# Four-layer graph network: one layer's count tables kept in DRAM for another layer, and a difference of two weights

## The reference

```
# L0, relation: 64 edge types
msg = (x[src] + rel_emb[type64]) @ W_msg.T + b_msg
agg = segment_sum(msg, dst) / max(deg, 1)
# L1, weighted attention, 4 heads: sums over edges grouped by src, weight edge_weight
# L2, typed: 2 edge types, 0 = data, 1 = control
m_data = Xs @ W_data.T + b_data           # Xs = X[src]
m_ctrl = Xs @ W_control.T + b_control
msg = where(type2 == 0, m_data, m_ctrl)
out = relu(segment_sum(msg, dst) + X @ W_self.T + b_self)
# L3, plain: h = x @ W.T + b, sums of norm * h[col] over edges and self loops
```

## Time and profile before

| what | us |
|---|---|
| median of three runs | 6132.15 (6131.38 to 6135.97) |
| the profiled execution | 6133.85 |
| its span in the profile | 6132.1 |
| sorting the edges, constants, L0's own projections (start to about 2256) | 2256 |
| L0: own stage | 2311 to 3084 |
| L1: own stage | 3173 to 4318 |
| L2: own stage, with its tail to 5524 | 4404 to 5501 |
| L3: own stage | 5568 to 6120 |

### The profile page before, as it was taken

How to read it: one execution, slowest core, us unless ns; L and a number is a source line. 1 busy time by engine, 2 the same in 40 slices (tenths; PEclk the granted TensorE clock), 3 DMA queues, 4 the chain that set the end, 5 groups by cost and what they waited for, 6 DMA issues and landing times. The chain is left out here.

```text
span 6132.1 us, 121790 instructions
## 1 busy us (share of the span) xinstructions
PE 5401.7 (88%) x44062; PEld 4317.7 (70%) x44063; DVE 4755.8 (78%) x12715; ACT 2193.0 (36%) x3365; POOL 1557.8 (25%) x1592
## 2 busy tenths in 40 slices
PE   4888888888888859999959999999699999997998
PEld 3666666666666646767659999999577777765666
DVE  7777777777777777788879999999555555557888
ACT  0111111111111114445423333333366666655665
POOL 0577777777777740000000000000000000000000
PEclk9999999999999989999979999999799999998999
DMA  2100000000000010000000000000000000000000
GB/s 79 24 2 2 2 2 2 2 2 2 2 2 2 2 35 4 2 1 2 1 3 1 1 1 1 1 1 1 2 1 1 1 1 1 1 1 2 7 8 10
DMA packets 60237, 33.64 MB, mean 5 GB/s; under 512 B 51583, under 2 KB 54097, under 8 KB 59598
## 3 DMA queue, kind: packets, MB, share of 16 engines
q1 hardware_dynamic: 8622, 22.14, 1.2%
q0 software_dynamic: 50176, 3.31, 0.9%
q10 hardware_dynamic: 1056, 2.86, 0.2%
HBM read 13.67 MB, written 14.54 MB: 5 GB/s over the span
## 5 line engine op out<-in xcount | busy, mean ns | idle before, releaser
L1391 ACT ACTIVATE gC<-qC 128x768 bf16<-128x768 f32 (+3 forms) x1960 | 1614.3, 824 | 1672.0 <-PE qC L1429 1667.0
L1530 PE MATMUL qO<-X,gC 128*128 128x384 bf16 x9604 | 1932.4, 326 | 8.7 <-ACT gC L1391 8.6
L596 POOL DMA_INDIRECT records<-rec,idx x1568 | 1548.6, 988 | 509.6 <-issue 493.4
L70 DVE TENSOR_TENSOR g<-iota_b,recs 128x768 bf16<-128x768 bf16 (+3 forms) x1970 | 1198.2, 644 | 537.8 <-PE qC L1429 526.6
L1429 PE MATMUL qC<-g 128*128 128x128 bf16 (+1 forms) x12029 | 1204.0, 242 | 45.8 <-DVE g L998 27.8
L1429 PEld LDWEIGHTS qC<-g 128*128 128x128 bf16 (+1 forms) x12029 | 1070.3, 136 | 207.3 <-DVE g L998 35.7
L1530 PEld LDWEIGHTS qO<-X,gC 128*128 128x128 bf16 x9604 | 889.1, 98 | 458.7 <-ACT gC L1391 13.3
L422 DVE SCALAR_TENSOR_TENSOR junk<-pK,key,earlier 128x128 f32<-128x128 f32 (+3 forms) x1568 | 768.2, 547 | 36.7 <-issue 34.5
L508 PE MATMUL pG<-run,hT 49*128 49x98 f32 x3136 | 793.4, 432 | 0.0
L508 PEld LDWEIGHTS pG<-run,hT 49*128 49x128 f32 x3136 | 697.1, 324 | 71.0 <-issue 71.0
L482 PE MATMUL pK<-ident_b,ts_b 128*128 128x128 bf16 x1572 | 379.7, 297 | 324.9 <-DVE junk L422 323.0
(11 more groups left out here) (278 smaller groups left out, 4397.8 us busy)
## 6 DMA issues: line engine op xcount, KB each, us to landing
records<-rec,idx POOLq DMA_INDIRECT x1568, 2.1
records<-null SPq DMA_DIRECT2D x31, 256.0 KB, 9.3
recs<-records SPq DMA_DIRECT2D x1, 4866.0 KB, 14.1
B<-in_x SPq DMA_DIRECT2D x1, 2744.0 KB
out<-B SPq DMA_DIRECT2D x7, 392.0 KB
ety<-in_edge_type ACTq DMA_DIRECT2D x2, 686.0 KB
esrc<-in_src SPq DMA_DIRECT2D x1, 686.0 KB
edst<-in_dst SPq DMA_DIRECT2D x1, 686.0 KB
```

The source lines that it names most:

```text
L70: return v.tensor_tensor(o.rearrange("p n (a b) -> p n a b", b=2), iota_b[:, 0:w].rearrange("p (a b) -> p a b", b=2).unsqueeze(1).broadcas ...
L596: gp.indirect_dma_start(rec_d, bass.IndirectOffsetOnAxis(ap=idx[:, k:k + 1], axis=0), rec[:, k, :], None).then_inc(s_sent[g % 2], 16)
L1391: act.activation(Cs[:, u % 2, 0:n, :], pC[u % 2][:, 0:n, :], ACT.Copy).then_inc(s_cs, 1)
L1530: mm = pe.matmul(pO[i % SUMS][:, 0:width], Cs[:, u % 2, j, :], x, start=first, stop=last)
```

## The change

- L0: the evacuated tables go to a ring of four buffers (`ring0`) in place of `gC`. A buffer holds a quarter of a destination tile's tables, two pieces (12 or 13 tables, 384 or 416 KB). When both pieces are in, SyncE stores the quarter to `tables` in DRAM, 196 stores in all. ScalarE waits, before it writes a buffer again, for the store of four quarters before (`s_tab`). L0's tables count all edges, data and control.
- L2: `H = 2` is gone; a piece has one table, that of the control edges (`g1` is 128 wide and compared with 128 to 255, `at=P`). SyncE loads L0's quarters into a ring of four buffers, two in `ring2` and two in `sl_f`, four at the start ahead of the weights and then each when the products of the quarter four before are done. TensorE waits for the quarter's load and multiplies L0's table with `X`, the control table with `X2`, both into `qO`.
- In L1's own stage, where L2's projections are made, the control weight and bias become the differences control minus data (two VectorE subtractions and a wait, `s_diff`), so that `X2` holds the control projection minus the data projection.
- L2's shared stage makes its 256-wide one-hot by two comparisons of 128, since its first half has to match edges of both types.

```
-            H = 2 if mode == "typed" else 1
...
+                if mode == "relation":
+                    ring = sb("ring0", [P, RING, LONGEST, P], BF16, c)
+                    kept = [ring[:, b, :, :] for b in range(RING)]
...
+                        if mode == "typed":
+                            for Q4 in range(RING):
+                                here, there = quarter(Q4)
+                                sp.dma_start(here, there).then_inc(s_tab[Q4 % RING], 16)
...
+                        if mode == "relation":
+                            for Q4 in range(NT * QUARTERS):
+                                here, there = quarter(Q4)
+                                sp.wait_ge(s_cs, 2 * Q4 + 2 + PRE)
+                                sp.dma_start(there, here).then_inc(s_tab[Q4 % RING], 16)
+                            for b in range(RING):
+                                sp.wait_ge(s_tab[b], 16 * (NT * QUARTERS // RING))
+                        if mode == "typed":
+                            for Q4 in range(RING, NT * QUARTERS):
+                                here, there = quarter(Q4)
+                                sp.wait_ge(s_o, 2 * (Q4 - RING) + 2 + PRE)
+                                sp.dma_start(here, there).then_inc(s_tab[Q4 % RING], 16)
...
-                                ins = equal(v, h1[:, par, 0:n, :], recs_h[:, own, H_SL:H_SL + 2], n, H * P)
+                                ins = equal(v, h1[:, par, 0:n, :], recs_h[:, own, H_SL:H_SL + 2], n, P, at=P if mode == "typed" else 0)
...
+                            if k == 2:
+                                v.tensor_tensor(wnat[:, 1, :], wnat[:, 1, :], wnat[:, 0, :], ALU.subtract).then_inc(s_diff, 1)
+                                v.tensor_tensor(bsrc[:, 1, :], bsrc[:, 1, :], bsrc[:, 0, :], ALU.subtract).then_inc(s_diff, 1)
+                                v.wait_ge(s_diff, 2)
...
+                                    if mode == "relation":
+                                        Q4 = i * QUARTERS + u // 2
+                                        if u % 2 == 0 and Q4 >= RING:
+                                            act.wait_ge(s_tab[Q4 % RING], 16 * (Q4 // RING))
+                                        act.activation(stored(i, u, 0, n), pC[u % 2][:, 0:n, :], ACT.Copy).then_inc(s_cs, 1)
...
+                                    if mode == "typed":
+                                        if q % 2 == 0:
+                                            Q4 = i * QUARTERS + q // 2
+                                            pe.wait_ge(s_tab[Q4 % RING], 16 * (Q4 // RING + 1))
+                                        for j in range(n):
+                                            a = cut[q] + j
+                                            pe.matmul(pO[i % SUMS][:, 0:width], stored(i, q, j, j + 1), X[:, a, :, :].rearrange("p s d -> p (s d)"), start=a == 0, stop=False)
```

More of the change, by code:

```diff
@@ L50, in gnn_four_layers_kernel @@
     rec_d = nc.dram_tensor("records", (P * NREC, REC // 4), F32, kind="Internal").ap()
+    QUARTERS = 4
+    LONGEST = max(NT * (r + 1) // QUARTERS - NT * r // QUARTERS for r in range(QUARTERS))
+    tab_d = nc.dram_tensor("tables", (NT * QUARTERS, P, LONGEST * P), BF16, kind="Internal").ap()
     with ExitStack() as ctx:
@@ L939, in aggregate_own @@
                 s_high = sem(f"n_high{name}", c) if k == 2 else None
+                s_diff = sem(f"n_diff{name}", c) if k == 2 else None
                 s_mid = sem(f"n_mid{name}", c) if k == 2 else None
@@ L943, in aggregate_own, with stored, quarter @@
                 LOADS = 16 * (2 * nW + nV)
+                s_tab = [sem(f"t_tab{name}{b}", c) for b in range(RING)] if by_source else None
+                def stored(i, q, lo, hi):
+                    at = cut[q] - cut[q // 2 * 2]
+                    return kept[(i * QUARTERS + q // 2) % RING][:, at + lo if hi == lo + 1 else slice(at + lo, at + hi), :]
+                def quarter(Q4):
+                    r = Q4 % QUARTERS
+                    n = cut[2 * r + 2] - cut[2 * r]
+                    return kept[Q4 % RING][:, 0:n, :].rearrange("p n d -> p (n d)"), tab_d[Q4, :, 0:n * P]
                 def pn(m, use):
@@ L1528, in batch @@
                                         if mode == "relation":
                                             pe.matmul(pR[:, 0:P], h3[:, q % NHB, j, :], h2[:, q % NHB, j, :], start=first, stop=last)
-                                        mm = pe.matmul(pO[i % SUMS][:, 0:width], Cs[:, u % 2, j, :], x, start=first, stop=last)
+                                        table_j = stored(i, q, j, j + 1) if mode == "relation" else Cs[:, u % 2, j, :]
+                                        mm = pe.matmul(pO[i % SUMS][:, 0:width], table_j, x, start=first, stop=last)
@@ L1531, in batch @@
                                     mm.then_inc(s_o, 1)
[L1532 to L1536, removed]
+                                    if m is not None:
+                                        node(m, tl, q)
+                                    elif (tl, q) == (1, 1):
+                                        weights()
```

56 lines of the change are left out of this document (32 added, 24 removed).

## The result

The changed kernel takes 5993.8 us, the median of four runs (5992.94 to 5997.61), beside 6131.76 for the kernel before (four runs, 6131.05 to 6135.97). The ratio is 0.9775, with a 95% interval of 0.9763 to 0.9787: 2.25% faster, or 138 us. The forecast was 6003 us, between 5992 and 6032.

What follows compares the result with a forecast made beforehand. L2's own stage was taken to be bound by TensorE's instruction stream. The terms -132 + 1 + 0.6 + 0.9 gave -129.5 us, so a median of 6003 us; own range 5996 to 6027, widened to 5992 to 6032.

Steps and rivals of the forecast that it cites:

- Tables: L2's TensorE stream: 2,401 table matmuls removed at 0.055 us each, 132 us saved, bounds 128 to 136.
- Evacuations and one-hots, "worth nothing": L2: ScalarE loses 392 evacuations and VectorE half the width of `g1`; both waited for PE, so no gain.
- Start of L2: L2's first products may wait for the first loaded quarters: +1 us taken, bounds 0 to +5.
- L2 as a whole: L2's own stage: 132 us of tables removed, +1 us at the start, nothing for evacuations, one-hots or later loads.
- Small additions: Two VectorE subtractions in L1, +0.6 us, and split comparisons in L2's shared stage, +0.9 us.
- Transfers priced at nothing: L0's stores and L2's later loads: 2.7 us each, hidden by 12.9 and 13.7 us of lead, so 0 us.
- the own range of the forecast: Whole kernel: the terms' bounds together, -136 to -105 us, giving 5996 to 6027 us.
- the first (a stream too slow): L0 and L2 wait on table transfers; a loss below 84 GB/s, about 6366 us on four DMA engines; chance 0.04.
- The second (TensorE held at the dense steps): L2: ScalarE's and VectorE's dense steps come late between shorter units, +48 us, 6051 us; chance 0.04.
- The third (traffic slows the engines): L0's and L2's loops: transfers slow the engines; at 3% +52 us, 6055 us; chance 0.05.
- The fourth (a table is worth its weight load of 98 ns): L2: weight loads set TensorE's pace, so 2,401 tables are worth 235 us, 5900 us; chance 0.01.
- the fifth (the time stays): L2: the time hangs on something else there and the kernel stays at 6132 us; chance 0.01.

Runs made afterwards that it cites:

- twice: Changed kernel, but L2 makes each control table twice into the same place; 6904.02 us on a chip with a slower sort, ratio 0.9989 to the kernel before.
- nonorm: Kernel before the change, with five of seven layernorm scalings per batch by ScalarE left out in L2; 6128.18 us, ratio 0.9993 to the kernel before.
- quiet: Changed kernel, storing and loading only the first four quarters, which L2 rereads; 6774.41 us on a chip with a slower sort, ratio 0.9808 to the kernel before.
- traffic2: Changed kernel, each quarter stored twice in L0 and copied once more in L2; 6767.6 us on a chip with a slower sort, ratio 0.9795 to before.
- traffic4: Changed kernel, each quarter stored four times in L0 and copied three times more in L2; 6024.17 us, ratio 0.9823 to the kernel before.
- ring2: Changed kernel with rings of two buffers in place of four; 6772.49 us on a chip with a slower sort, ratio 0.9804 to the kernel before.

## Why the prediction was right, step by step

- **Tables: 132 us taken, 133 to 134 measured.** The distance of 0.055 us was read from rows rounded to 0.01. From piece to piece it is (2.62 - 2.285) / 6 = 0.0558 us, and with the work put back (twice) 0.0554; twice has no wait for the first quarter, which makes its figure a little low. That is 133 to 134 us, inside the bounds of 128 to 136. By the Trainium skill's 81 ns per matmul ("TensorE: Matmul & The Clock Gate", section "Back-to-back issue gap") it would have been 194; twice shows that this does not hold for this stream.
- **Evacuations and one-hots, "worth nothing": this step was too low by about 5 us**, and it is the largest error in the sum. The argument was that both engines wait for PE, with 3.3 us the other way. Those 3.3 us, 7 times, stood in the rows that I had chosen. The same lateness, seen at the weight loads, has a row that I left out:

```profile
PEld qO L1530 <- ACT gC L1391: 5.8, 13, 0.7
```

The two are not to be added; the lengths of the late units give 5.3 us. I took the 3.3 us for nothing because they are small beside 1097. They are not small beside the other terms. The kernel after has no such wait and no unit of 2.00 us. nonorm shows 4.3 us of them by themselves; the other microsecond, from the 1.50 us units, is read from their length only.
- **Start of L2: +1 taken, +0.8 found.** Up to the loop's plain pace the stage loses 2.57 us before and 3.37 after. The wait for the first quarter is real, 0.77 us. Its products began 3.8 us after the load went out, later than a landing of 2.7 us would have it, but well short of the +2.3 that the prediction gives for a start that needs all four quarters; the +1 chosen between the two was about right.
- **L2 as a whole.** -134 - 5.3 + 0.8 = -138.5, and the traces differ by 138.6. The forecast for this part was -131.
- **Small additions: +1.5 taken, +1.8 found** from L0's first table to L2's, where the traces of kernels with the change scatter by a microsecond (2093.7 to 2094.8). L1's two subtractions take 0.28 and 0.27 us. L1's loop, from first table to last product, is 1145.2 us in after and 1143.9 to 1145.2 in the other kernels with the change, against 1143.4 in both traces without it: 0.5 to 1.8 us more, where 0.6 was forecast. L2's shared stage has twelve comparisons of 418 ns in place of the six of 685, and they reach 15.1 us from first to last instead of 14.5; 0.3 of the 0.9 us arrived at L2's first table.
- **Transfers priced at nothing: right.** quiet and traffic2 show the same loops with none and with twice of them. Landings were put at 2.7 us and are 2.3 for stores and 3.0 to 3.2 for loads. The 301 GB/s of the earlier trace rows was a weak support for the rate: it is a window of one microsecond, and other such windows of that trace read up to 623 GB/s with a DMA share above 1, so they are no rate to rely on. The capacity is what traffic4 shows over 798 us.
- **From sum to number.** The sum gave -129.5. The right sum is -138.5 + 1.8 - 0.9 = -137.6, 8 us further. The median moved by 138.0, to 5993.8, near the lower end of the range: the own range of the forecast (5996 to 6027) misses it by 2 us. Its bounds leaned to the wrong side. They allowed 24 us for what might get worse and 7 us for what might get better, most of that for the rounding of the tables' price. Only the wider range that was stated (from 5992) holds the result.

Of the rivals, the first (a stream too slow) needs a rate below 84 GB/s; traffic4 puts the capacity above 390. The clock in L2 stood at 1.00. The second (TensorE held at the dense steps) went the other way: with a shorter stream no product of L2 waits for ScalarE, which lost 319 us of work there where TensorE lost 134. The third (traffic slows the engines) is refuted at one, two and, in L2, four times the traffic. The fourth (a table is worth its weight load of 98 ns) falls with twice, and the fifth (the time stays) with the result. What the change would bring with a second core streaming from the same memory was not tried.

## What to carry to other kernels

A stage in which one engine never stands is a sum of starts: take the distance from one start to the next, not the duration of an instruction, and count. Where work is taken off the other engines too, look in the waits for the few times that they held up the bound engine; the row is small, but it goes as a whole and belongs in the sum. A result that one stage leaves can be kept in DRAM and read back at next to no cost: here the ring's lead (13 us) was several times a landing (3 us) and the rate (83 to 104 GB/s) well under what the DMA engines moved (393), and only the first load of the stage was seen. Even a lead of one quarter (ring2) cost under 3 us.

## What the runs showed of the hardware

- **The DMA engines beside busy compute engines.** One queue, fed by SyncE with transfers of 384 and 416 KB, moved 393 GB/s over L0's loop, and no engine's instructions became longer by it (matmuls 326, 219 and 220 ns, evacuations 810 ns against 809, one-hots 552 and 553 ns against 550 and 552). I had expected about 350.
- **Landings grow before throughput ends.** A load of 384 KB lands in 3.1 us alone, 4.0 with the transfers doubled, 6.5 with four times of them; L2's loop does not notice (957.2 to 958.5 us in quiet, traffic2 and traffic4).
- **TensorE's clock in the sort.** In the profiled execution of the kernel after, the granted clock was 0.50, its level of 1.2 GHz, through the stretches below, where the kernel before had 1.00 with the same busy shares:

```profile
1000.00:1100.00 100.00, 83.35 (x473) 65.89 (x472) 79.86 (x274) 15.88 (x42) 75.21 (x77) 0.50 0.03 2
2000.00:2100.00 100.00, 83.58 (x468) 66.33 (x468) 78.93 (x271) 17.45 (x43) 74.83 (x79) 0.50 0.03 2
```

The sort took 2308.1 us in it against 2311.1, and the other executions of the same kernel, at 0.97 over the span, took the same time. One of 13 executions of the kernel before shows it as well, 0.81 over the span and 6128.73 us, where the median is 6132.75. So up to L0, TensorE's speed is not what counts, and the clock of that stretch says nothing of the result. What made it fall there I can't say.
- **A chip on which the sort takes some 760 us longer.** Behind the sort, variants of the changed kernel took the same there as the changed kernel here, within 1.3 us (quiet, traffic2). Compare stages, not totals, between chips.
